# Top-6 routing of a one-core Trainium2 kernel rewritten: eight largest logits taken straight from PSUM, chosen ids marked in a row of ids, row addresses by one more top-eight

## The chip, the cores and the metric

The kernel runs on one core of one Trainium2 chip. The metric is the device time of one execution in microseconds; lower is better.

## The reference

The program is two gated blocks of two layers each, over x of shape (8, 256, 512), all in float32. The last layer is a mixture of experts, and the change is in its routing. Cut to what matters:

```python
x = x + tanh(g_xattn[0]) * retention(layernorm(x), ctx)      # stages F.*
x = x + tanh(g_ffn[0]) * dense_ffn(layernorm(x))             # stages F.*
x = x + tanh(g_xattn[1]) * attention(layernorm(x), ctx)      # stages T.*, L.*: 8 heads, softmax over 512
# the routed layer (stages R.*, L.*, then the experts); E = 64 experts, TOPK = 6, CAP = 256 rows per expert
scores = sigmoid(x_flat @ w_gate)                            # (2048, 64)
_, topk_idx = top_k(scores, 6)
w = take_along_axis(scores, topk_idx, -1); w = w / w.sum(-1, keepdims=True)
pos = (running count of earlier choices of the same expert)  # valid = pos < 256
x_disp[expert, pos] = x_flat[token]                          # dropped where pos >= 256
h = silu(g_r) * v_r;  out_r = h @ w_down[expert]
routed = sum over the 6 choices of w * out_r[expert, pos] (0 where dropped)
x = x + tanh(g_ffn[1]) * (shared_mlp(x) + routed)
```

## The kernel before, in words

Tokens come in 8 batches of 256 (two tiles of 128 partitions each). The program has three parts. `setup_and_scores` (to about 72 us in the profile) makes the retention matrix. `main_loop` (72 to 790 us) runs three pipelines over the batches at once: F (retention and dense layer), T (attention, key by key group) and R (normalisation, gate logits and routing). `experts` (790 us to the end) goes through 32 pairs of experts and then adds the results.

The order of the work on every engine is written out by hand in two tables, `ORDER` and `ENDING`. An entry `R.gates+2` in ORDER means: in step s, do stage R.gates for batch s-2. There are 7 steps, s = 0 to 6; after them ENDING lists the rest as stage/batch. Every engine walks the same list and runs the entries for which it has code, strictly in that order. So an entry's place also decides what stands behind it in each engine's queue. In step s the tables hold F for batch s, T for batch s-1 (from s = 1) and R for batch s-2 (from s = 2), so R runs inside steps 2 to 6 for batches 0 to 4; batches 5, 6 and 7 are in ENDING, and batch 7 is split into its two tiles (stages L.*).

Names that the prediction uses:
- `quad` is four PSUM banks. `T.S0` to `T.S7` write attention scores there on TensorE (line 1279), and after each one VectorE takes a maximum over 2,048 columns (`maxima`, L992, tile t_nmx). `QUADS` makes T.S(n+1) wait on TensorE until that maximum is done. `T.Q0` to `T.Q7` (L1319, L1322) write the shifted scores there again, and ScalarE takes the exponential (L791, L802).
- `T.sum0a`, `T.sum0b`, ... on GpSimd add exponentials, four additions of 128x512 each (L703, tile t_psum). Additions and indirect DMAs (`R.x0` to `R.x3`, L715, which send rows to their expert's slots in xs_d) share GpSimd's queue.
- Routing before: `R.gates` (TensorE, logits; ScalarE takes exp(-logit) over 128x128), `R.sigmoid` on VectorE (add 1, reciprocal, MAX8 and FIND_INDEX8 per tile, cast of the ids), `R.hot` (a one-hot of 6 x 64 per token by comparison with a row of ids, its sum over the six choices, the running count `cum`), `R.pos` on TensorE (prefix sums by two small matmuls per tile), `R.slots` (the one-hot times the positions, and a reduction) and `R.places` (address = a packing of expert and position, with a large number added for dropped rows; token ids; weights).
- L.* are the same stages for batch 7, one tile at a time; `L.up0` to `L.up7` (TensorE, L1186) are the shared expert's first matmuls, kept to fill the end of the main loop.

## Time and profile before

| | us |
|---|---|
| timed runs, median of 3 | 1126.71 (1125.02 to 1128.56) |
| profiled execution, first to last instruction | 1137.7 |
| TensorE busy, VectorE busy in it | 1041.9, 681.7 |
| GpSimd busy, ScalarE busy in it | 485.5, 322.6 |

The only time that the profiled execution has of its own is its span, 1137.7 us; that is 11.0 us above the median of the timed runs. The engines overlap, so their busy times do not add up to the span. PE is TensorE, PEld its weight loads, DVE VectorE, ACT ScalarE, POOL GpSimd.

### The profile page before, as it was taken

The page shows a single profiled execution, that of the slowest core. Times are in us where ns is not written, and L with a number is a line of the kernel's source. Part 1 is how long each engine was busy: PE and PEld are TensorE (multiplying, and loading weights), DVE is VectorE, ACT ScalarE, POOL GpSimd, SP SyncE. Part 2 cuts the span into 40 slices and gives each one's busy share as a digit, 9 for nine tenths or more (in the row PEclk, how much of TensorE's full clock was granted, in tenths as well). Part 3 has the DMA queues.
Part 4 walks back from the last instruction along what each step waited for, and adds up shares of the span by engine and source line. Part 5 has one row for each costly group of instructions (what it writes and reads, how often), then busy time and mean ns, then how long its engine had stood idle before and what let it go on. Part 6 is the DMA issues. An engine that isn't in the chain of part 4 may idle for free.

```text
span 1137.7 us, 16279 instructions
## 1 busy us (share of the span) xinstructions
PE 1041.9 (92%) x6109; PEld 570.0 (50%) x6110; DVE 681.7 (60%) x1290; ACT 322.6 (28%) x446; POOL 485.5 (43%) x468
## 2 busy tenths in 40 slices
PE   7988889999999999999999987789999999998586
PEld 6975544554454554545544622347555555554232
DVE  3331463778878787787788755763444444443366
ACT  3420023224133232232241321432433333333121
POOL 1100013625655665647657485054344454445100
PEclk9997999999999999999999996899999999999799
DMA  8872079579580580661603141436879999983898
GB/s 310 298 312 93 1 268 375 192 289 336 184 327 30 187 316 20 243 241 65 217 1 113 77 156 73 182 133 256 301 286 392 374 366 341 376 290 140 330 409 321
DMA packets 93786, 262.30 MB, mean 231 GB/s; under 512 B 10623, under 2 KB 10751, under 8 KB 92944
## 3 DMA queue, kind: packets, MB, share of 16 engines
q1 hardware_dynamic: 43920, 146.18, 35.1%
q10 hardware_dynamic: 31872, 63.97, 15.2%
q0 software_dynamic: 17920, 51.15, 11.5%
q8 instruction: 48, 0.79, 0.3%
q14 instruction: 26, 0.21, 0.1%
HBM read 129.91 MB, written 139.72 MB: 237 GB/s over the span
## 4 chain that ended last, share of the span: by engine, by line
PE 76%; DMA 7%; DVE 6%; issue 4%; ACT 3%; POOL 3%; another core or an unknown queue 1%; SPq 0%; POOLq 0%; ACTq 0%; DVEq 0%
PE banks L1178 18%; PE banks L1186 10%; PE banks L1687 10%; PE banks L1279 6%; PE banks L1319 6%; PE banks L1698 6%; DMA e_eo<-y_d 6%; PE banks L1673 6%; PE banks L1337 4%; DVE t_nmx L992 3%; PE banks L1200 2%; ACT t_probs L791 1%; PE banks L1172 1%; POOL t_psum L703 1%; PE banks L391 1%
## 5 line engine op out<-in xcount | busy, mean ns | idle before, releaser
L1526 POOL DMA_INDIRECT y_d<-e_eo,e_ids x128 | 124.5, 972 | 148.4 <-DVE e_eo L1615 117.2
L992 DVE TENSOR_REDUCE t_nmx<-banks 128x4 f32<-128x2048 f32 x64 | 146.4, 2288 | 55.0 <-PE banks L1279 54.9
L703 POOL TENSOR_TENSOR t_psum<-t_psum,t_probs 128x512 f32<-128x512 f32 x112 | 140.8, 1289 | 63.0 <-ACT t_probs L791 61.5
L791 ACT ACTIVATE t_probs<-banks 128x2048 f32<-128x2048 f32 x56 | 105.1, 1878 | 149.6 <-PE banks L1322 139.0
L715 POOL DMA_INDIRECT xs_d<-r_norm,r_xaddr x96 | 96.5, 1005 | 52.1 <-DVE r_xaddr L1125 26.5
L1279 PE MATMUL banks<-b_key,b_qry 32*128 32x512 f32 x512 | 77.1, 673 | 25.4 <-DVE t_nmx L992 19.0
L675 POOL TENSOR_TENSOR f_rstd<-f_veps,mhalf 128x2 f32<-128x2 f32 x24 | 16.9, 706 | 189.1 <-DVE f_veps L893 189.0
L1319 PE MATMUL banks<-b_qry,b_key 32*128 32x512 f32 x512 | 73.9, 647 | 16.0 <-ACT t_probs L791 7.3
L703 POOL TENSOR_TENSOR t_psum<-t_probs,t_probs 128x512 f32<-128x512 f32 x56 | 72.0, 1319 | 16.3 <-ACT t_probs L791 14.3
L1673 PE MATMUL banks<-ident,e_xg 128*128 128x128 f32 x512 | 70.4, 280 | 1.6 <-DMA e_xg<-xs_d 0.9
L1673 PEld LDWEIGHTS banks<-ident,e_xg 128*128 128x128 f32 x512 | 54.8, 141 | 26.2 <-issue 24.3
L1591 DVE COPY e_xT<-banks 128x512 f32<-128x512 f32 x44 | 30.4, 692 | 58.4 <-PE banks L1673 57.9
L1186 PE MATMUL banks<-f_normT,wupT 128*128 128x256 f32 x256 | 63.5, 405 | 0.0
L1178 PE MATMUL banks<-wo,f_zT 128*128 128x512 f32 x128 | 60.3, 616 | 2.4 <-issue 2.4
L1615 DVE COPY e_eo<-banks 128x512 f32<-128x512 f32 x64 | 44.3, 692 | 27.7 <-PE banks L1698 20.1
L1337 PE MATMUL banks<-t_probs,b_cT 128*32 128x512 f32 x448 | 60.6, 625 | 0.0
L1186 PE MATMUL banks<-b_xnT,wg 128*128 128x256 f32 x256 | 59.9, 389 | 0.2 <-DVE f_zT L912 0.2
L1186 PEld LDWEIGHTS banks<-f_normT,wupT 128*128 128x128 f32 x256 | 50.4, 202 | 17.6 <-issue 10.5
L1178 PE MATMUL banks<-wdnT,f_hT 128*128 128x512 f32 x128 | 58.8, 604 | 0.0
L1178 PE MATMUL banks<-wexp,f_normT 128*128 128x512 f32 x128 | 58.5, 601 | 0.0
L1546 ACT ACTIVATE e_eo<-banks 128x512 f32<-128x512 f32 x64 | 38.2, 597 | 62.7 <-PE banks L1698 43.6
L1186 PEld LDWEIGHTS banks<-b_xnT,wg 128*128 128x128 f32 x256 | 48.5, 194 | 12.4 <-issue 5.6
(217 smaller groups left out, 1653.8 us busy)
## 6 DMA issues: line engine op xcount, KB each, us to landing
xs_d<-zero ACTq DMA_DIRECT2D x32, 1056.0 KB, 9.9
e_xg<-xs_d SPq DMA_DIRECT2D x32, 1056.0 KB
y_d<-zero ACTq DMA_DIRECT2D x24, 1024.0 KB
e_xg<-y_d SPq DMA_DIRECT2D x16, 768.0 KB, 15.1
e_eo<-y_d SPq DMA_DIRECT2D x16, 768.0 KB, 14.5
wo<-in_wud SPq DMA_DIRECT2D x8, 768.0 KB
wupT<-in_wud SPq DMA_DIRECT2D x8, 768.0 KB
wdnT<-in_wud SPq DMA_DIRECT2D x8, 768.0 KB
```

The lines of the kernel that those rows point to most:

```text
L703: ins = g_.tensor_tensor(psum0[:, q, :], first[:, q, :], probs[s % NP][:, q, :], ALU.add)
L715: g_.indirect_dma_start(out=xs_d, out_offset=bass.IndirectOffsetOnAxis(ap=xaddr[b % 2][:, t, k:k + 1], axis=0), in_=normR[b % 2][:, t, :], ...
L791: A(probs[s % NP][:, :, :], quad[:, :, :], ACT.Exp, scale=SCALE1).then_inc(W["exp_ok"], 1)
L992: V.tensor_reduce(nmx[g][:, m, :], quad[:, :, :], axis=AX.X, op=ALU.max, negate=True).then_inc(W["mx_ok"], 1)
L1178: ins = mm(dst, lhs[:, k, t * P:(t + 1) * P], w[:, k, :], start=(k == 0), stop=(k == KC - 1))
L1186: ins = mm(dst[:, j * S:(j + 1) * S], w[:, k, o * P:(o + 1) * P], rhs[:, k, :], start=(k == 0), stop=(k == KC - 1))
L1279: ins = mm(quad[:, q, :], qry[b % 2][r, g, m * P:(m + 1) * P], key[b % 2][r, g, :], start=True, stop=True)
L1319: mm(quad[:, q, :], key[b % 2][r, g, n * P:(n + 1) * P], qry[b % 2][r, g, :], start=True, stop=False)
L1337: ins = mm(pV[q * HD:(q + 1) * HD, :], cT[:, n, r:r + HD], probs[s % NP][:, q, :], start=(n == 0), stop=(n == KC - 1))
L1526: g_.indirect_dma_start(out=y_d, out_offset=bass.IndirectOffsetOnAxis(ap=ids[:, HC * p + n:HC * p + n + 1], axis=0), in_=eo[u][:, n, :], i ...
L1673: last = tr(pT[t][:, k * P:(k + 1) * P], xg[u][:, HT * e + t, k * P:(k + 1) * P], ident[:, :])
L1687: last = mm(pU[j][HE * e:HE * (e + 1), 0:CAP], wu[u][:, e, k, j * HE:(j + 1) * HE], xT[p % 3][:, e, k, :], start=(k == 0), stop=(k == KC - 1))
```

## The change

It rewrites the routing stages, moves them in the two tables and changes how rows are addressed. It does the following.

- `R.sigmoid` and `R.hot` become one VectorE stage `R.top`. MAX8 and FIND_INDEX8 read the logits in PSUM (the sigmoid keeps their order, so the same six are found). The ids are cast, and MATCH_REPLACE writes -1 over the chosen ids in a row of 72 ids (64 experts and 8 fillers); "below 0" then gives the 0/1 row `chosen16`, and also `room`, a constant per expert where it is chosen. The running count is updated from `chosen16`; a third small matmul per batch replaces one of its two copies.
- `R.slots` becomes: subtract the positions from `room`, zero what does not fit, MAX8, and one tensor_scalar that turns the result into addresses. The six addresses of a token now come sorted by expert, and an expert's rows are filled in plain order (256 x expert + position) where they were interleaved in two halves.
- `R.places` goes; `R.weigh` takes exp(-x) of eight values per token (ScalarE, at R.pos), and VectorE makes sigmoid, sum and weights of those.
- Token ids are written once at the start by GpSimd (4 iotas) and raised by one VectorE instruction per batch (`next_tokens`, behind R.norm) from batch 2 on.
- In ORDER, R.top stands behind F.turn2B and ahead of T.S5; R.sigmoid had stood behind F.upA and R.hot behind F.upB. In ENDING, R.x0 and R.x1 of batch 6 both stand ahead of L.add0, and slots of tile 0 stand ahead of norm of tile 1.

```diff
-T.S5+1 R.x3+3 T.V0+1 F.logits+0 T.V1+1 F.best+0 T.S6+1 F.upA+0 R.sigmoid+2 T.S7+1 T.P1+1 F.upB+0 R.hot+2 T.Q2+1 F.weight+0 T.M1+1
+R.norm+2 F.x1b+0 T.Q0+1 R.turnA+2 F.stats2+0 R.turnB+2 R.keep+2 F.next+0 R.x2+3 T.Q1+1 T.sum0a+1 R.gates+2 F.turn2A+0 F.norm2+0 F.turn2B+0 R.top+2
+T.S5+1 R.x3+3 T.V0+1 F.logits+0 T.V1+1 F.best+0 T.S6+1 F.upA+0 T.S7+1 T.P1+1 F.upB+0 T.Q2+1 F.weight+0 T.M1+1
...
+        pool.wait_ge(at_done, 4)
+        for u in range(2):
+            g_.iota(tokk[u], pattern=[[TOPK * P, T], [1, TAG]], base=u * TOPK * S - NOWHERE, channel_multiplier=TOPK,
+                    allow_small_or_imprecise_dtypes=True).then_inc(W["zero_ok"], 1)
...
+        def next_tokens(b):
+            V.tensor_scalar(tokk[b % 2], tokk[b % 2], float(2 * TOPK * S), None, ALU.add)
...
+        def r_top(part):
+            def stage(b):
                 each, ts, n = tiles(b, part)
+                if b == 0:
+                    dve.wait_ge(W["zero_ok"], 6)
+                dve.wait_ge(W["gt_mm"], n)
+                p = lambda t: bank("R.gates", b)[:, t * E1:(t + 1) * E1] if part is None else bank(f"L.gates{t}", b)[:, 0:E1]
                 for t in each:
+                    ins = V.max(top[:, t, :], p(t))
                 link("r", ins)
                 for t in each:
+                    ins = V.max_index(topi[:, t, :], top[:, t, :], p(t))
+                ins.then_inc(W["top_ok"], 1)
+                dve.wait_ge(W["top_ok"], n)
+                link("r", V.tensor_copy(topf[b % 2][:, ts, 0:TOPK], topi[:, ts, 0:TOPK]))
+                for t in each:
+                    ins = V.match_replace(out=marked[:, t, :], in_to_replace=topf[b % 2][:, t, :], in_values=iota_e[:, :], imm_value=-1.0)
+                if part != 1:
+                    V.tensor_copy(cum16[:, :], cum[:, :])
                 link("r", ins)
+                V.tensor_scalar(chosen16[:, ts, :], marked[:, ts, 0:E1], 0.0, None, ALU.is_lt).then_inc(W["m_ok"], 1)
+                ins = V.scalar_tensor_tensor(out=room[:, ts, :], in0=marked[:, ts, 0:E1], scalar=0.0,
+                                             in1=place_e[:, :].unsqueeze(1).broadcast_to([P, len(each), E1]), op0=ALU.is_lt, op1=ALU.mult)
+                link("r", ins)
+                if part is None:
+                    for t in each:
+                        link("r", V.tensor_tensor(cum[:, :], cum[:, :], chosen16[:, t, :], ALU.add))
...
+                link("r", V.tensor_tensor(left[:, ts, :], room[:, ts, :], p, ALU.subtract))
+                V.scalar_tensor_tensor(out=slot[:, ts, :], in0=p, scalar=float(CAP), in1=left[:, ts, :], op0=ALU.is_lt, op1=ALU.mult).then_inc(W["pos_ok"], 1)
...
+                    ins = V.max(slot8[:, t, :], slot[:, t, :])
...
+                V.tensor_scalar(xaddr[u][:, ts, :], slot8[:, ts, 0:TOPK], -1.0, float(ROWS_END), ALU.mult, ALU.add).then_inc(W["route_ok"], 1)
...
+                if t == 1:
+                    mm(dst[:, t * E1:(t + 1) * E1], ones16[:, :], chosen16[:, 0, :], start=False, stop=False)
+                ins = mm(dst[:, t * E1:(t + 1) * E1], ones16[:, :], cum16[:, :], start=False, stop=True)
```

On VectorE, in a middle step of the main loop, these rows stand in the program before, from the second normalisation of F (f_norm) to the first conversion of the attention maxima (t_nmp). The three TENSOR_REDUCE rows are the maxima of T.S5, T.S6 and T.S7:

```order
L935 TENSOR_SCALAR f_norm<-f_xs_74,f_mv,f_rstd 128x512 x2
L992 TENSOR_REDUCE t_nmx<-banks 128x4
L942 MAX f_m<-banks 128x8 x2
L944 TENSOR_TENSOR f_gap<-f_m 128x2
L992 TENSOR_REDUCE t_nmx<-banks 128x4
L1066 TENSOR_SCALAR r_eg<-r_eg 128x128
L1067 RECIPROCAL r_score<-r_eg 128x128
L1069 MAX r_top<-r_score 128x8 x2
L1072 MAX_INDEX r_topi<-r_top,r_score 128x8 x2
L1074 CAST r_norm_79<-r_topi 128x2x8
L992 TENSOR_REDUCE t_nmx<-banks 128x4
```

And this stands at the same place of VectorE's queue in the changed program:

```order
L939 TENSOR_SCALAR f_norm<-f_xs_74,f_mv,f_rstd 128x512 x2
L1077 MAX r_top<-banks 128x8 x2
L1080 MAX_INDEX r_topi<-r_top,banks 128x8 x2
L1083 CAST r_norm_79<-r_topi 128x2x6
L1085 MATCH_REPLACE r_marked<-r_norm_79,iota_e 128x72 x2
L1087 CAST r_cum<-r_cum 128x64
L1089 TENSOR_SCALAR r_chosen<-r_marked 128x128
L1090 SCALAR_TENSOR_TENSOR r_room<-r_marked,place_e 128x128
L1095 TENSOR_TENSOR r_cum<-r_cum,r_chosen 128x64 x2
L996 TENSOR_REDUCE t_nmx<-banks 128x4
L946 MAX f_m<-banks 128x8 x2
L948 TENSOR_TENSOR f_gap<-f_m 128x2
```

The routing instructions moved from behind the maximum of T.S6 to the front of the maximum of T.S5, and what R.hot did later in the step now stands here too.

On GpSimd, near the end of the main loop, these rows stand in the program before, from batch 6's residual sum (r_acc_76) to batch 7's first one-tile power (r_rstd 128x1); the DMA rows send batch 6's rows to xs_d, twelve of them in all:

```order
L711 TENSOR_TENSOR r_acc_76<-f_xs_73,t_att 128x512
L680 TENSOR_TENSOR r_rstd<-r_veps,mhalf 128x2
L715 DMA xs_d<-r_norm_78,r_xaddr 16384x528 x3
L711 TENSOR_TENSOR r_acc_77<-f_xs_74,t_att 128x512
L715 DMA xs_d<-r_norm_78,r_xaddr 16384x528 x3
L685 TENSOR_TENSOR r_rstd<-r_veps,mhalf 128x1
```

In the changed program the same stretch of GpSimd's queue reads:

```order
L718 TENSOR_TENSOR r_acc_76<-f_xs_73,t_att 128x512
L687 TENSOR_TENSOR r_rstd<-r_veps,mhalf 128x2
L722 DMA xs_d<-r_norm_78,r_xaddr 16384x528 x6
L718 TENSOR_TENSOR r_acc_77<-f_xs_74,t_att 128x512
L692 TENSOR_TENSOR r_rstd<-r_veps,mhalf 128x1
```

Batch 7's first residual sum now stands behind six sends of batch 6 instead of three, and none stand between it and the power.

## Rows read from the trace of the kernel before

**Rows 1.** Page, part 1: busy us, share of the span, instructions.

```profile
PE 1041.9 (92%) x6109; PEld 570.0 (50%) x6110; DVE 681.7 (60%) x1290; ACT 322.6 (28%) x446; POOL 485.5 (43%) x468
```

**Rows 2.** Windows: stretch, length, busy by engine (instructions), granted clock, DMA share, GB/s.

```profile
359.00:437.50 78.50, 76.05 (x455) 38.75 (x453) 61.86 (x107) 22.95 (x25) 47.78 (x43) 1.00 0.50 183
640.00:645.00 5.00, 5.00 (x19) 4.03 (x16) 4.07 (x9) 0.00 (x0) 0.97 (x1) 0.66 0.27 108
757.00:790.00 33.00, 29.80 (x130) 24.87 (x130) 15.39 (x57) 5.22 (x10) 17.04 (x17) 0.90 0.50 185
790.00:1047.00 257.00, 253.43 (x1790) 141.97 (x1792) 120.48 (x295) 91.45 (x168) 117.65 (x121) 1.00 0.87 325
```

**Rows 3.** Waits of TensorE, 359.0 to 437.5 us: total, times, longest.

```profile
PE banks L1279 <- DVE t_nmx L992: 1.4, 1, 1.4
PE banks L1319 <- ACT t_probs L791: 1.0, 1, 1.0
```

**Rows 4.** Groups of VectorE by shape: count, busy us, mean ns, idle before.

```profile
L1104 DVE TENSOR_TENSOR r_ohp<-r_onehot,r_post 128x384 f32<-128x384 bf16 x16 | 19.3, 1238 | 1.4 <-DVE r_post L1101 1.4
...
L1084 DVE TENSOR_REDUCE r_chosen<-r_onehot 128x128 f32<-128x768 bf16 x7 | 10.5, 1497 | 0.2
```

**Rows 5.** Timeline, 395 to 410 us (step 4): start, us, instruction, idle before.

```profile
396.14 2.00 PE L1178 MATMUL banks<-wg,r_normT 128*128 128x64 f32 x16
...
399.56 4.94 POOL L703 TENSOR_TENSOR t_psum<-t_probs,t_probs 128x512 f32<-128x512 f32 x4
...
400.22 2.29 DVE L992 TENSOR_REDUCE t_nmx<-banks 128x4 f32<-128x2048 f32 x1 [3.67 <-PE banks L1279]
...
403.28 1.25 DVE L944 TENSOR_TENSOR f_gap<-f_m 128x2 f32<-128x2 f32 x1
403.89 1.14 PE L1279 MATMUL banks<-b_key,b_qry 32*128 32x512 f32 x8
...
405.10 2.29 DVE L992 TENSOR_REDUCE t_nmx<-banks 128x4 f32<-128x2048 f32 x1 [0.56 <-PE banks L1279]
...
408.55 0.35 DVE L1069 MAX8 r_top<-r_score 128x8 f32<-128x64 f32 x2
...
408.94 0.09 DVE L1072 MATCH_VALUE_LOAD r_topi<-r_top,r_score 128x8 f32 x1
...
409.21 0.22 DVE L1072 FIND_INDEX8 r_topi<-r_top,r_score 128x8 uint32<-128x64 f32 x1
409.46 0.17 DVE L1074 CAST r_norm<-r_topi 128x16 f32<-128x16 uint32 x1
```

**Rows 6.** Timeline, 648 to 655 us: small VectorE operations beside GpSimd's additions.

```profile
648.89 4.93 POOL L703 TENSOR_TENSOR t_psum<-t_probs,t_probs 128x512 f32<-128x512 f32 x4 [7.76 <-ACT t_probs L791]
649.34 0.90 DVE L1085 CAST r_chosen<-r_chosen 128x128 bf16<-128x128 f32 x1
650.16 1.27 DVE L1089 CAST r_cum<-r_cum 128x64 bf16<-128x64 f32 x1
...
651.35 1.33 DVE L1090 TENSOR_TENSOR r_cum<-r_cum,r_chosen 128x64 f32<-128x64 f32 x1
...
652.72 1.17 DVE L1089 CAST r_cum<-r_cum 128x64 bf16<-128x64 f32 x1
653.81 0.21 DVE L1090 TENSOR_TENSOR r_cum<-r_cum,r_chosen 128x64 f32<-128x64 f32 x1
```

**Rows 7.** Timeline, 239 to 250 us (step 2).

```profile
239.10 2.00 PE L1178 MATMUL banks<-wg,r_normT 128*128 128x64 f32 x16
...
241.25 4.95 POOL L703 TENSOR_TENSOR t_psum<-t_probs,t_probs 128x512 f32<-128x512 f32 x4 [3.14 <-ACT t_probs L791]
...
246.86 1.14 PE L1279 MATMUL banks<-b_key,b_qry 32*128 32x512 f32 x8
```

**Rows 8.** Timeline, 784 to 791 us: the end of the main loop.

```profile
789.28 0.60 ACT L867 ACTIVATE r_normT<-banks 128x512 f32<-128x512 f32 x1 [2.86 <-PE banks L1186]
...
790.12 1.06 PE L1673 MATMUL banks<-ident,e_xg 128*128 128x128 f32 x8 [0.88 <-DMA e_xg<-xs_d]
```

More of the change, by code:

```diff
@@ L31 @@
 SCALE1 = float(1.0 / np.sqrt(np.float32(HD)))
-SKIP = 1.0e6
+ROWS_END = 1 << 15
 NOWHERE = 1 << 20
@@ L442 @@
 F.turnA/7 T.V7/5 T.Z1/5 F.turnB/7 T.add1/5 T.S3/6 F.gateA/7 R.x0/4 R.stats/5 F.gateB/7 R.x1/4 T.S4/6 T.P0/6 F.keys/7 R.acc/5 F.x1a/7
-R.norm/5 T.S5/6 T.M0/6 F.x1b/7 R.turnA/5 R.turnB/5 F.stats2/7 F.next/7 R.x2/4 T.Q0/6 F.norm2/7 R.gates/5 T.S6/6 F.turn2A/7 F.turn2B/7 T.V0/6
-R.x3/4 T.sum0a/6 F.logits/7 T.S7/6 R.sigmoid/5 T.sum0b/6 T.P1/6 F.upA/7 T.Q1/6 T.sum0c/6 F.upB/7 F.best/7 T.Q2/6 R.hot/5 F.weight/7 T.M1/6
-F.expert0/7 R.slots/5 R.places/5 R.x0/5 R.pos/5 T.Q3/6 T.V1/6 F.down0/7 R.keep/5 T.Q4/6 F.expert1/7 T.Q5/6 R.x1/5 F.down1/7 T.V2/6 L.load/7
+R.norm/5 T.S5/6 T.M0/6 F.x1b/7 R.turnA/5 R.turnB/5 F.stats2/7 F.next/7 R.x2/4 T.Q0/6 F.norm2/7 R.gates/5 T.S6/6 R.top/5 F.turn2A/7 F.turn2B/7 T.V0/6
@@ L446 @@
+R.x3/4 T.sum0a/6 F.logits/7 T.S7/6 T.sum0b/6 T.P1/6 F.upA/7 T.Q1/6 T.sum0c/6 F.upB/7 F.best/7 T.Q2/6 F.weight/7 T.M1/6
+F.expert0/7 R.slots/5 R.weigh/5 R.x0/5 R.pos/5 T.Q3/6 T.V1/6 F.down0/7 R.keep/5 T.Q4/6 F.expert1/7 T.Q5/6 R.x1/5 F.down1/7 T.V2/6 L.load/7
 T.Q6/6 F.stats3/7 T.V3/6 T.Z0/6 F.norm3/7 R.x2/5 T.Q7/6 T.V4/6 T.cT/7 R.acc/6 T.A0/6 R.x3/5 L.S0/7 T.sum1a/6 T.V5/6 T.V6/6 L.S1/7 T.add0/6
-L.S2/7 L.S3/7 T.sum1b/6 L.up0/7 L.S4/7 T.V7/6 L.P0/7 T.sum1c/6 L.S5/7 T.A1/6 L.M0/7 T.add1/6 T.Z1/6 L.Q0/7 R.stats/6 R.x0/6 L.Q1/7 R.norm/6
@@ L579, in main_loop @@
     tokk = [normR[u][:, :, D + TAG:XW] for u in range(2)]
[L580 to L581 removed]
+    marked = sb("r_marked", [P, T, E1 + TAG])
     chosen16 = sb("r_chosen16", [P, T, E1], BF16)
     cum = sb("r_cum", [P, E1])
[L584 to L588 removed]
+    cum16 = sb("r_cum16", [P, E1], BF16)
+    room = sb("r_room", [P, T, E1])
+    left = sb("r_left", [P, T, E1])
+    slot = sb("r_slot", [P, T, E1])
+    slot8 = sb("r_slot8", [P, T, 8])
+    etop = sb("r_etop", [P, T, 8])
+    sig = sb("r_sig", [P, T, 8])
     wsum = sb("r_wsum", [P, 2, T])
@@ L614, in main_loop, with tiles @@
     last = lambda b, t: b + 1 + t
+    def tiles(b, t):
+        return (range(T), slice(0, T), b + 1) if t is None else ((t,), slice(t, t + 1), last(b, t))
     def load_front(sp, b):
@@ L817, in r_turn, with r_exps @@
             return stage
-        def r_gates(b):
-            act.wait_ge(W["gt_mm"], b + 1)
-            A(eg[:, :, :], bank("R.gates", b)[:, 0:T * E1].rearrange("p (t e) -> p t e", t=T), ACT.Exp, scale=-1.0).then_inc(W["eg_ok"], 1)
+        def r_exps(part):
+            def stage(b):
+                each, ts, n = tiles(b, part)
+                act.wait_ge(W["top_ok"], n)
+                A(etop[:, ts, :], top[:, ts, :], ACT.Exp, scale=-1.0).then_inc(W["etop_ok"], 1)
+            return stage
         def last_turn(t):
@@ L1047, in stage @@
                                 ALU.subtract, ALU.mult).then_inc(W["x4n_ok"], 1)
+                if t == 0:
+                    next_tokens(b)
             return stage
@@ L1132, in vector @@
                   "F.stats3": f_stats3, "F.norm3": f_norm3, "T.P0": parts(0), "T.P1": parts(1), "T.A0": attended(0), "T.A1": attended(1),
-                  "R.stats": r_stats, "R.norm": r_norm, "R.sigmoid": r_sigmoid(None), "R.hot": r_hot(None),
-                  "R.slots": r_slots(None), "R.places": r_places(None),
+                  "R.stats": r_stats, "R.norm": r_norm, "R.top": r_top(None), "R.slots": r_slots(None), "R.weigh": r_weigh(None),
                   "L.P0": parts(0), "L.P1": parts(1), "L.A0": attended(0), "L.A1": attended(1)}
@@ L1142, in vector @@
             stages[f"L.norm{t}"] = last_norm(t)
-            stages[f"L.sigmoid{t}"] = r_sigmoid(t)
-            stages[f"L.hot{t}"] = r_hot(t)
+            stages[f"L.top{t}"] = r_top(t)
             stages[f"L.slots{t}"] = r_slots(t)
-            stages[f"L.places{t}"] = r_places(t)
+            stages[f"L.weigh{t}"] = r_weigh(t)
         for n in range(KC * NG):
```

131 lines of the change are left out of this document (42 added, 89 removed), and 2 rows, old and new, of the table RELEASES.

## The prediction

> **What bounds the kernel now.** I read the page's busy times first, then the windows of single stretches, then the waits inside one step, then the timeline around the place where the routing moves to. Over the span TensorE is busy 92% and VectorE 60% [rows 1]. That average hides the stages, so the windows come next: in the step from 359.0 to 437.5 us TensorE works 76.05 of 78.50 us at the full granted clock, VectorE 61.86 [rows 2]. What is left to TensorE is 2.4 us of waits, and the list of waits names both: 1.4 us for the maximum of one quad (t_nmx) and 1.0 us for one exponential [rows 3]. Both are the round trip of a quad that TensorE has just written and needs again; neither waits for routing. In the expert stage TensorE is busy 253.43 of 257.00 us [rows 2]. So the kernel is bound by TensorE, and VectorE matters only where TensorE stands still for it.
>
> **What the change removes.** Three of the instructions that go, two products of one-hot and positions at 1,238 ns on average and one reduction at 1,497 ns [rows 4], already make 2 x 1.24 + 1.50 = 4.0 us of VectorE per batch. The rest of R.hot, R.slots and R.places adds to that. I cost this at nothing: in the middle steps TensorE hides it, with no wait for it in the list [rows 3]. If a step were bound by VectorE the same edit would be worth those 4 us and more; there is none. The large exponential on ScalarE goes and a small one comes at a place where ScalarE has idle time; also nothing. The one extra small matmul per batch (64 columns) has no row of its own; I bound it by 0 and by one sixteenth of the gate group of the same width (2.00 us for sixteen fp32 matmuls [rows 5]), 0.13 us; eight batches make 0 to 1.0 us, and I take 0.2, since nothing waits for its result.
>
> **What it moves, and what that costs.** R.top now stands ahead of the maximum of T.S5 in VectorE's queue. TensorE cannot start T.S6 until that maximum is done. The timeline of step 4 gives the room [rows 5]. The gate logits end at 396.14 + 2.00 = 398.14. The maximum of S5 ran from 400.22 for 2.29 us, to 402.51, and TensorE came to T.S6 at 403.89 without waiting. VectorE had been idle for 3.67 us before 400.22, and that gap is where R.top is put. The slack: R.top may end at 403.89 - 2.29 = 401.60, that is 3.46 us after the logits, before TensorE waits.
>
> How long is R.top on a quiet chip? Two MAX8 0.35 us (SBUF source in the row; PSUM now, taken the same). FIND_INDEX8 with its loads, twice: 408.94 to 409.43, 0.49. Cast of ids 0.17. MATCH_REPLACE is not in this trace; below nothing it cannot be, above I bound it by the FIND pair, which also loads eight values and streams a row of about this length, and take that, 0.49. Then a cast of the count, the comparison, `room` and two additions: 0.21 each by the last row of [rows 6], 1.05. With five hand-overs of 0.03 (409.43 to 409.46 [rows 5]) it is 2.7 us, ending at 400.8. That fits, with 0.8 to spare.
>
> But it is not quiet there. GpSimd's four additions of T.sum0a run from 399.56 to 404.50 [rows 5], right over the second half of R.top. What such company does to a small VectorE instruction is shown at 648.89 [rows 6]. There four additions run in 4.93 us, 1.23 us each. The cast that starts at 649.34 ends at 650.24, the next cast takes 1.27 us, an addition of 64 columns 1.33, another cast 1.17, and the same addition takes 0.21 once GpSimd has finished. So each of them passes only when one GpSimd instruction ends, one per GpSimd instruction. The f_gap row in step 4 itself (1.25 us for two columns [rows 5]) ends at 404.53, at the end of the same four additions. The maxima from PSUM are not touched: 2.29 us beside these additions.
>
> Now R.top in step 4 with this rule. MAX8, FIND, cast: 398.14 + 0.35 + 0.49 + 0.17 + 0.1 = 399.25. MATCH_REPLACE reads one row; I take it as unhindered: 399.75. The cast of the count then meets the first addition, the comparison the second, `room` the third, the first cum addition the fourth, ending at 404.50; the second cum addition is free, 0.26 with its hand-over: 404.76. The maximum of S5 ends at 407.05, TensorE starts T.S6 at 407.1 instead of 403.89. **A stall of 3.2 us.** It is robust against small shifts: there are five instructions to pass and four additions to pass them at, so one of them slipping in early changes only who is last. What is queued behind: on VectorE the maximum, then F's logits (f_gap), not needed by TensorE at once; on TensorE T.S6, the up projection, everything after. TensorE has no spare time in the step to win it back.
>
> Steps 3 to 6 have the same pattern: 4 x 3.2 = 12.8. Step 2 (batch 0) has its additions from 241.25 to 246.20, right behind logits that end at 241.10, and T.S6 at 246.86 [rows 7]. Cast of ids, cast of count, comparison and `room` each meet one; the two cum additions follow free, 0.5, so R.top ends at 246.7, the maximum at 249.0: 2.2 us. Together 15.0 us. From batch 2 on next_tokens (bounded by 0 and 0.2, the small-instruction row) stands ahead of F's statistics and moves sum0a later by as much: 3 x 0.2 = 0.6.
>
> The Trainium skill has the rule behind the row: SBUF — State Buffer, section Who interferes with whom, says that VectorE's copies, casts and tensor_scalars in a two-port mode, and any instruction with two SBUF inputs, wait for a whole GpSimd instruction, while reductions and one-input instructions outside those modes never do. By that, `room` and the comparison wait as I assumed and MATCH_REPLACE does not; the trace agrees for casts and additions, and shows nothing for the other three. Without these sentences the sum is the same.
>
> **The clock.** A stall of 3 us can also lower TensorE's granted clock. The windows show one such place: at 640 to 645 us, in the same part of a step (T.S7 and the up projection behind the narrow logits), it is 0.66 over 5 us [rows 2], which is 5 x 0.34 = 1.7 us of full-clock work lost, and that without a stall. Whether the new stall does it no row shows: 0 to 5 x 1.7 = 8.5 us. I take 3, nearer nothing, since step 4 as it stands keeps 1.00 through its own two waits.
>
> **The ends of the main loop.** Batch 5's R.top (ENDING) stands behind the maximum of T.S6; GpSimd adds only from 648.89 there [rows 6], so it runs free. For batch 7 addresses come earlier, and so do the last sends. But TensorE begins the experts at 790.12, and the last copy it also needs ends at 789.28 + 0.60 = 789.88 [rows 8]. So rows that land 2 or 3 us earlier buy 0.2 us, unless the shared matmuls in front get faster too. TensorE is idle 33.00 - 29.80 = 3.2 us in that stretch at clock 0.90 [rows 2]; I take -0.7, from 0 to -6.5 (3.2 idle and 3.3 of clock). The four iotas stand where GpSimd waits; 0. Rows in plain order in xs_d change neither bytes nor matmuls; 0.
>
> **Sum.** 15.0 + 0.6 + 0.2 + 3 - 0.7 = 18.1 us. Against the profiled execution: 1137.7 to about 1155.8. The timed runs lie 11.0 below that; the shift should carry over: 1126.7 + 18.1 = 1144.8, I say **1145 us**, slower.
>
> **Rivals.**
> (a) As above, stall of about 3 us in five steps, clock between nothing and 8.5: 1126.7 + 15.8 - 0.7 = 1142 up to 1150, with margins 1138 to 1154. Chance 0.55. For it: [rows 6] and the place in [rows 5].
> (b) Only casts and additions wait, comparison and `room` do not: then three instructions meet three additions, R.top ends near 403.3, the maximum at 405.6, a stall of 1.7 to 1.9: five make 9, 1130 to 1138. Chance 0.15. Against it: nothing direct.
> (c) No stall: VectorE gets its instructions through, or TensorE meets slack. R.top ends at 400.8, under the 401.60 that decides. What stays is the end of the loop: 1126. Chance 0.15. Against it: f_gap at the same place does wait.
> (d) Faster, the other side: no stall, and the end of the loop pays. R.top ends before 401.60, batch 7's prefix matmul finds its input ready, the shared matmuls follow without a gap and the clock stays up from 757 to 790 us: up to 6.5 us, 1120 to 1123. Chance 0.15. For it: TensorE is idle 3.2 us there. Against: the up matmuls alone fill most of it.
> A fifth case, that the change does not shorten VectorE's work, is excluded by the 4.0 us of instructions gone.
>
> **How the numbers follow.** About 0.3% (3.4 us) is what a measurement of this kernel can tell from no change. Slower by more: (a) and (b), 0.70. Within: (c), 0.15. Faster: (d), 0.15. The time is that of (a), 1145, whose own range is 1138 to 1154. The range for 8 in 10 leaves out most of (d) and what lies above 1154: 1123.5 to 1154.
>
> **What would show it.** Right: in steps 2 to 6 TensorE's wait for t_nmx (T.S6 behind T.S5) once more per step, about 3 us, at T.S6; five VectorE instructions of about 1.2 us between the gate logits and that maximum, while sum0a runs; VectorE's busy time in a step clearly down from 61.86 although the step is longer (81 to 83 us against 78.50); TensorE's start of the experts bound by the last shared copy. Wrong: R.top in under 3.4 us, steps of 78.5 us, or comparison and `room` at 0.2 beside the additions (b). What would upset all of it is GpSimd starting sum0a later than R.top ends.

## The result and the profile after the change

The changed kernel takes 1166.37 us (median of 4 runs, 1165.27 to 1167.46), the kernel before 1126.71 us in the same comparison (median of 3; a fourth execution, of 1245.04 us, was in a slow state and is left out). The ratio is 1.0355, with a 95% interval of 1.0335 to 1.0375. That is 39.7 us slower. The direction was forecast and so was the place; the size was not: 18.1 us were predicted, and 1166 lies 12 us above the top of the range.

Page of the changed kernel, part 1 (against [rows 1]):

```profile
PE 1058.5 (91%) x6117; PEld 580.6 (50%) x6118; DVE 624.6 (54%) x1216; ACT 321.6 (28%) x446; POOL 484.3 (42%) x471
```

VectorE lost 57 us of busy time, as its code lost instructions (an instruction of VectorE that is held counts as busy here, so the instructions saved more than that), and TensorE's busy time grew by 16.6 us with 8 matmuls more: the same work was done at a lower clock. The windows of the five steps that hold routing, cut at the first matmul of F.out0, show where (columns as in [rows 2]). First the changed kernel, then the control, which is the kernel before run once more:

```profile
204.11:287.70 83.59, 78.80 (x458) 40.21 (x454) 53.09 (x98) 22.84 (x25) 35.35 (x31) 0.96 0.71 265
...
373.31:458.75 85.44, 78.43 (x458) 39.94 (x454) 55.78 (x99) 22.83 (x25) 47.55 (x43) 0.96 0.46 168
...
sum 426.94, PE 393.81 PEld 200.38 DVE 277.89 ACT 114.80 POOL 227.17; mean PE 78.76 PEld 40.08 DVE 55.58 ACT 22.96 POOL 45.43
```

```profile
201.23:280.13 78.90, 76.16 (x456) 38.77 (x452) 60.49 (x107) 22.96 (x25) 35.62 (x31) 1.00 0.78 281
...
358.66:437.19 78.53, 76.08 (x456) 38.77 (x453) 61.88 (x107) 22.97 (x25) 47.83 (x43) 1.00 0.49 183
...
sum 394.57, PE 381.84 PEld 194.27 DVE 309.92 ACT 115.47 POOL 228.67; mean PE 76.37 PEld 38.85 DVE 61.98 ACT 23.09 POOL 45.73
```

Steps 2 to 6 together take 426.94 - 394.57 = 32.4 us more, 4.7 in step 2 and 6.8 to 7.1 in each of the others. In step 4 VectorE is busy for 55.78 us where it was for 61.88, and the step is longer by 6.9. The waits of TensorE in that step name the cause (against [rows 3]):

```profile
PE banks L1273 <- DVE t_nmx L996: 6.0, 2, 4.6
```

The wait for the maximum of a quad, 1.4 us before, is 6.0 now (the one for the exponential is still 1.0), 4.6 of it in one place. The timeline there (step 4, against [rows 5]):

```profile
410.54 2.00 PE L1172 MATMUL banks<-wg,r_normT 128*128 128x64 f32 x16
...
413.06 0.97 POOL L722 DMA_INDIRECT xs_d<-r_norm,r_xaddr  x1 [0.30 <-issue]
...
413.51 5.52 DVE L1083 CAST r_norm<-r_topi 128x12 f32<-128x12 uint32 x1
...
414.04 4.95 POOL L710 TENSOR_TENSOR t_psum<-t_probs,t_probs 128x512 f32<-128x512 f32 x4
...
419.34 0.22 DVE L1085 MATCH_REPLACE8 r_marked<-r_norm,iota_e 128x72 f32<-128x72 f32 x1
...
420.57 2.29 DVE L996 TENSOR_REDUCE t_nmx<-banks 128x4 f32<-128x2048 f32 x1
...
422.92 2.09 PE L1273 MATMUL banks<-b_key,b_qry 32*128 32x512 f32 x8 [4.56 <-DVE t_nmx L996]
```

One instruction does it. The cast of 12 ids, which takes 0.17 us on a quiet chip ([rows 5]), begins 0.53 us before GpSimd's four additions and ends with the last of them. The prediction had it end before them. Everything behind the cast is then quick. Behind the stall of 4.56 us the T.S6 matmuls take 2.09 us instead of 1.14, because the clock has fallen:

```profile
415.00:420.00 5.00, 3.36 (x32) 2.02 (x24) 4.97 (x8) 0.00 (x0) 4.84 (x5) 1.00 1.00 359
420.00:425.00 5.00, 2.08 (x9) 0.58 (x9) 3.08 (x7) 0.20 (x1) 2.09 (x3) 0.58 1.05 409
425.00:430.00 5.00, 5.00 (x21) 3.96 (x23) 2.29 (x1) 0.02 (x1) 0.00 (x0) 0.74 1.04 406
```

The granted clock (third column from the end) goes to 0.58 and 0.74, that is, part of the time at the lower of the two levels, 1.2 GHz, after TensorE had stood still.

Step 2 went as forecast, because there the additions run already when the cast comes:

```profile
243.48 4.96 POOL L710 TENSOR_TENSOR t_psum<-t_probs,t_probs 128x512 f32<-128x512 f32 x4 [3.13 <-ACT t_probs L798]
...
244.37 0.41 DVE L1083 CAST r_norm<-r_topi 128x12 f32<-128x12 uint32 x1
...
245.10 0.22 DVE L1085 MATCH_REPLACE8 r_marked<-r_norm,iota_e 128x72 f32<-128x72 f32 x1
...
245.96 1.34 DVE L1089 TENSOR_SCALAR r_chosen<-r_marked 128x128 bf16<-128x128 f32 x1
247.22 1.37 DVE L1090 SCALAR_TENSOR_TENSOR r_room<-r_marked,place_e 128x128 f32<-128x128 f32 x1
...
251.49 2.09 PE L1273 MATMUL banks<-b_key,b_qry 32*128 32x512 f32 x8 [2.34 <-DVE t_nmx L996]
```

Each of the cast, the count (245.24, 0.81 us), the comparison and `room` passes at the end of one addition, MATCH_REPLACE is not touched, and TensorE stalls 2.34 us.

### The profile page after: what moved, and what is told of

The parts are those of the page before. It is cut to its first block, busy times and chain, and to the rows that moved or that the text cites. A ratio compares the mean times of both kernels' runs of the same rounds, so it can differ in the third digit from the quotient of the medians.

```text
span 1165.7 us, 16200 instructions
## 1 busy us (share of the span) xinstructions
PE 1058.5 (91%) x6117; PEld 580.6 (50%) x6118; DVE 624.6 (54%) x1216; ACT 321.6 (28%) x446; POOL 484.3 (42%) x471
## 4 chain that ended last, share of the span: by engine, by line
PE 78%; DVE 10%; DMA 6%; ACT 3%; issue 2%; POOL 1%; SPq 0%; POOLq 0%; ACTq 0%; DVEq 0%
PE banks L1172 17%; PE banks L1180 13%; PE banks L1685 10%; PE banks L1273 6%; PE banks L1313 6%; PE banks L1696 6%; PE banks L1671 5%; DMA e_eo<-y_d 5%; DVE t_nmx L996 4%; PE banks L1331 3%; PE banks L1194 2%; DVE r_norm L1083 2%; ACT t_probs L798 2%; PE banks L395 1%; PE banks L389 1%
## 5 line engine op out<-in xcount | busy, mean ns | idle before, releaser
L1273 PE MATMUL banks<-b_key,b_qry 32*128 32x512 f32 x512 | 83.0, 721 | 45.5 <-DVE t_nmx L996 40.2
L1180 PE MATMUL banks<-f_normT,wupT 128*128 128x256 f32 x256 | 68.8, 429 | 0.0
L1180 PEld LDWEIGHTS banks<-f_normT,wupT 128*128 128x128 f32 x256 | 54.5, 218 | 23.4 <-issue 15.0
L1273 PEld LDWEIGHTS banks<-b_key,b_qry 32*128 32x128 f32 x512 | 21.9, 200 | 81.0 <-DVE t_nmx L996 56.3
L1613 DVE COPY e_eo<-banks 128x512 f32<-128x512 f32 x64 | 44.3, 692 | 29.4 <-PE banks L1696 29.4
```

The source lines that it names most:

```text
L1180: ins = mm(dst[:, j * S:(j + 1) * S], w[:, k, o * P:(o + 1) * P], rhs[:, k, :], start=(k == 0), stop=(k == KC - 1))
L1273: ins = mm(quad[:, q, :], qry[b % 2][r, g, m * P:(m + 1) * P], key[b % 2][r, g, :], start=True, stop=True)
```

## The experiments

**Control.** The kernel before, again. It gives the step lengths above and the spread of one execution.

> The kernel before, unchanged, as a control. Every theory expects the ratio 1.000 and, in a profile without a disturbed stretch, a span about 10 us under the 1137.7 us profiled before (in which TensorE stood still around 675 to 700 us, a stall that the changed kernel's profile does not have), steps of 78.5 us.

Measured: 1128.15 us, ratio 1.0003 [0.9979, 1.0027]; the profiled execution spans 1131.9 us. Single executions of this kernel run from 1123 to 1134 us (on the chip of one later run, from 1133 to 1150), so only differences of steps are read from single profiles below, and times from medians.

**The additions later.** In ORDER only:

```diff
-... R.x2+3 T.Q1+1 T.sum0a+1 R.gates+2 ... R.top+2 T.S5+1 R.x3+3 T.V0+1 ...
+... R.x2+3 T.Q1+1 R.gates+2 ... R.top+2 T.S5+1 R.x3+3 T.sum0a+1 T.V0+1 ...
```

> The changed kernel with GpSimd's four sum0a additions issued behind the send R.x3 in the main loop, so that the new routing stage runs beside sends alone. Theory A (the company of the four additions is what holds the new stage): the cast of the ids takes 0.2 us, the stage ends 2.7 us after the logits, steps 3 to 6 are 78 to 79 us, TensorE's clock stays at 1.00 in them, and the time is 1126 to 1132 us. Theory B (the stage is long by itself, or its place ahead of the maximum costs whatever GpSimd does): steps stay at 85 us and the time at 1160 to 1166 us. Under A a rest is possible if the additions, being later, hold something else: about 1 to 3 us per step.

Measured: 1145.89 us, ratio 1.0173 [1.0153, 1.0194]: half of the loss is gone, which is less than A had allowed for. Steps 3 to 6 are still 2.2 to 3.8 us longer than in the control, and step 2 is still 4.7 us longer: there is no send in it, so the edit changes nothing there and the stage meets the additions as before. In steps 3 to 6 the new stage is free of the additions (the ids' cast takes 0.17 us), but another instruction took its part:

```profile
407.78 5.17 DVE L948 TENSOR_TENSOR f_gap<-f_m 128x2 f32<-128x2 f32 x1
407.97 4.94 POOL L710 TENSOR_TENSOR t_psum<-t_probs,t_probs 128x512 f32<-128x512 f32 x4
...
415.20 1.67 PE L1273 MATMUL banks<-b_key,b_qry 32*128 32x512 f32 x8 [2.05 <-DVE t_nmx L996]
```

A subtraction of 2 columns asks 0.19 us before the additions and waits 5.17 us, in all four of steps 3 to 6. It now holds the maximum behind it, and TensorE 2.05 us later. So it is neither the cast nor its type: it is what GpSimd does at that moment. The cast itself begins here 0.36 to 0.46 us into a send, as it does in the changed kernel, but another send follows and not the additions, and it passes:

```profile
403.14 0.98 POOL L722 DMA_INDIRECT xs_d<-r_norm,r_xaddr  x1 [0.30 <-issue]
...
403.57 0.17 DVE L1083 CAST r_norm<-r_topi 128x12 f32<-128x12 uint32 x1
```

**The send later.** `T.Q1+1 T.sum0a+1 R.x2+3` instead of `R.x2+3 T.Q1+1 T.sum0a+1`, so that GpSimd is adding when the cast comes.

> The changed kernel with the send R.x2 issued behind the sum0a additions, so that GpSimd is already inside an addition when VectorE comes to the cast of the ids. Theory A1 (the cast waits through all four additions because it is requested just before they begin, behind a send): the cast then takes at most 1.3 us, each small instruction passes at the end of one addition, the stall is the 2 to 3.2 us per step of the prediction, steps 82 to 84 us, time 1140 to 1152 us. Theory A2 (the cast of 12 unsigned integers waits for a run of additions wherever it meets them): the cast again takes about 5 us, or what is left of the four additions, steps 84 to 86 us and 1160 to 1168 us.

Measured: 1155.27 us, ratio 1.0240 [1.0208, 1.0272]. The mechanism is A1's (the cast was held because it asked behind a send, just before the additions):

```profile
407.46 4.96 POOL L710 TENSOR_TENSOR t_psum<-t_probs,t_probs 128x512 f32<-128x512 f32 x4 [2.69 <-ACT t_probs L798]
...
408.28 0.48 DVE L1083 CAST r_norm<-r_topi 128x12 f32<-128x12 uint32 x1
409.21 0.81 DVE L1087 CAST r_cum<-r_cum 128x64 bf16<-128x64 f32 x1
```

The same cast takes 0.48 us, the comparison and `room` behind it 1.34 and 1.37, one to an addition. The stall at T.S6 is 2.33 to 2.35 us in steps 2 to 6, and steps 3 to 6 are 82.5 to 84.2 us, as expected. The time came out 3 us above the range: the five steps are 22.5 us longer than the control's, and the rest of the 29.4 us (against 1125.83) lies outside them and is not explained. The edit changes two things at once: the cast asks during the first addition, and no send stands directly ahead of the additions any more. This run is the prediction's own mechanism, one instruction to an addition. Of its 22.5 us, 11.7 are stalls and 10.8 come on top of them.

**One cast alone.** The kernel before with a stage of constant data at the new stage's place; its own routing untouched:

```diff
+        def r_probe(b):
+            dve.wait_ge(W["gt_mm"], b + 1)
+            for t in range(T):
+                ins = V.max(q_m[:, t, :], iota_e[:, :])
+            link("r", ins)
+            for t in range(T):
+                ins = V.max_index(q_i[:, t, :], q_m[:, t, :], iota_e[:, :])
+            link("r", ins)
+            link("r", V.tensor_copy(q_f[:, :, :], q_i[:, :, 0:TOPK]))
```

> The kernel before, with four instructions more on VectorE where the changed kernel has its routing stage (behind the gate logits, ahead of the maximum of T.S5): two top-eights, two searches for ids and ONE cast of 12 unsigned integers, all of constant data; its own routing is untouched. Theory A (a two-port instruction that asks for SBUF while the last send of GpSimd runs and four additions stand right behind it waits for all four): the cast takes 5.5 us in steps 3 to 6, TensorE then waits 4.0 to 4.6 us for the maximum, and with the clock's share steps are 84 to 85 us: this one cast makes the kernel 1150 to 1158 us. Theory B (the loss of the changed kernel is made by the whole stage, by its ten or so instructions one after another): a single cast costs at most 1.3 us, which the slack holds: steps 78.5 to 79 us, 1126 to 1129 us.

Measured: 1152.33 us against 1128.01, ratio 1.0205 [1.0181, 1.0229], +24.3 us.

```profile
402.27 5.41 DVE L1140 CAST q_f<-q_i 128x12 f32<-128x12 uint32 x1
402.70 4.94 POOL L704 TENSOR_TENSOR t_psum<-t_probs,t_probs 128x512 f32<-128x512 f32 x4
...
410.06 2.09 PE L1290 MATMUL banks<-b_key,b_qry 32*128 32x512 f32 x8 [2.91 <-DVE t_nmx L993]
```

One cast, held in steps 3 to 6, costs 24 us, where the whole change costs 39.7. The stall was 2.91 to 3.13 us where 4.0 to 4.6 was expected, for want of the 1.5 us of small work that stands behind the cast in the changed kernel. Step 2 is as before (78.90 us): there the cast takes 0.50 us and the slack holds it.

**The same cast 0.9 us earlier.** The same stage without the two top-eights and searches.

> The kernel before with the one cast of 12 unsigned integers again at the place of the new routing stage, but without the top eights and the searches ahead of it, so that it asks 0.9 us earlier: about 1.3 us before the first of the four additions, at the end of the send before the last or between the two. Theory A (only a request that comes within the last send, after GpSimd has the additions next, is held for all four): the cast takes 0.2 us, or up to 0.5 if it meets a send, steps 3 to 6 are 78.5 us, 1124 to 1131 us, ratio 0.998 to 1.003. Theory B (whoever asks while GpSimd sends is held until its additions are over): the cast takes 6 to 7 us, the steps are 84 us and the time 1150 us. That is the same instruction as in the run with the cast alone, 0.9 us earlier.

Measured: 1143.15 us against 1140.50 for the kernel before on that chip, ratio 1.0015 [0.9979, 1.0051]: no change.

```profile
394.88 0.97 POOL L717 DMA_INDIRECT xs_d<-r_norm,r_xaddr  x1 [0.31 <-issue]
395.76 0.17 DVE L1137 CAST q_f<-q_i 128x12 f32<-128x12 uint32 x1 [1.64 <-PE banks L1186]
396.16 0.97 POOL L717 DMA_INDIRECT xs_d<-r_norm,r_xaddr  x1 [0.30 <-issue]
397.14 4.95 POOL L705 TENSOR_TENSOR t_psum<-t_probs,t_probs 128x512 f32<-128x512 f32 x4
```

It asks inside a send and passes at once, 1.38 us before the additions. In step 3 it asks 0.26 us before the end of that send, takes 0.26 us and ends with it. So a send can hold a cast to its own end, but not beyond it when another send follows. In step 2, where GpSimd is idle, the cast asks only 0.11 us before the additions, and passes too:

```profile
238.76 0.17 DVE L1137 CAST q_f<-q_i 128x12 f32<-128x12 uint32 x1 [1.99 <-PE banks L1186]
...
238.87 4.95 POOL L705 TENSOR_TENSOR t_psum<-t_probs,t_probs 128x512 f32<-128x512 f32 x4 [3.14 <-ACT t_probs L793]
```

So neither a send alone nor nearness to the additions alone holds a request for 5 us. What the held requests of steps 3 to 6 share is a send with the additions directly behind it.

**Does the end of an instruction let it in?** Two versions of the changed kernel: a memset of one column ahead of the additions, and a hand-over between them.

```diff
+                if n == 1 and g == 0:
+                    g_.memset(q_t[:, :], 0.0)
```

```diff
                     ins = g_.tensor_tensor(psum0[:, q, :], first[:, q, :], probs[s % NP][:, q, :], ALU.add)
+                    if n == 1 and g == 0 and q < G - 1:
+                        ins.then_inc(W["q_add"], 1)
+                        pool.wait_ge(W["q_add"], (G - 1) * b + q + 1)
```

> The changed kernel with a memset of one element per partition on GpSimd between the send and the first of the four additions. Theory A1 (what matters is that the additions stand directly behind the send; a GpSimd instruction's end lets VectorE in): the cast passes behind the memset or the first addition, 0.5 to 2 us, and the others one per addition, as in the run with the send moved back: steps 82 to 83.5 us, 1148 to 1157 us. Theory A2 (whoever asks before a run of back-to-back GpSimd instructions waits for the whole run): the cast again takes about 5.6 us, steps 85.5 us, 1166 us.

> The changed kernel with a hand-over between the four additions of sum0a (each raises a semaphore that GpSimd itself waits for before the next), so that they are no longer back to back. Theory A3 (a request that came before the run waits because no gap opens in it): the cast passes at the first gap, about 1.8 us after its start, and the rest one per addition: steps 82 to 84 us. Theory A4 (the request waits for something else, such as the last addition's own end): the cast still takes 5.5 us or slightly more, steps 85.5 to 86 us, 1166 to 1170 us.

Measured: with the memset 1166.23 us (1.0325 [1.0301, 1.0348]); with the hand-overs 1159.16 us (1.0273 [1.0242, 1.0305]). First the one, then the other:

```profile
414.32 5.54 DVE L1086 CAST r_norm<-r_topi 128x12 f32<-128x12 uint32 x1
414.81 0.12 POOL L711 MEMSET q_t<- 128x1 f32 x1
414.87 4.94 POOL L713 TENSOR_TENSOR t_psum<-t_probs,t_probs 128x512 f32<-128x512 f32 x4
```

```profile
408.49 1.86 DVE L1086 CAST r_norm<-r_topi 128x12 f32<-128x12 uint32 x1
409.01 5.32 POOL L710 TENSOR_TENSOR t_psum<-t_probs,t_probs 128x512 f32<-128x512 f32 x4
```

The end of the memset did not let the cast in: it waits through all five, as A2 says. (The memset's record ends 0.06 us after the first addition's begins, so there was no gap at that end.) With gaps of some 0.12 us ((5.32 - 4.95) / 3) it passes at the first, as A3 says. So this cast needs a gap in the run of additions.

Is that because it asked early, or because the additions stand directly behind a send? The versions so far changed both together. The profile of the version with the cast 0.9 us earlier has a place, near the end of the main loop, that parts them:

```profile
679.99 0.97 POOL L717 DMA_INDIRECT xs_d<-r_norm,r_xaddr  x1 [0.30 <-issue]
680.98 4.92 POOL L705 TENSOR_TENSOR t_psum<-t_probs,t_probs 128x512 f32<-128x512 f32 x4
681.31 5.16 DVE L1023 SCALAR_TENSOR_TENSOR t_att<-t_att,tg_x,r_ohp 128x512 f32<-128x512 f32 x1
```

This instruction, 0.79 us at a free place of the control, asks 0.33 us after the first addition has begun, and still all four end before it does. In step 3 of the control, f_gap asks 3.55 us into such a run, 0.2 us before the third addition ends, and is held to the end of the fourth (1.44 us). So asking early is not what matters. Nothing that waited got in between additions that stand directly behind a send. The runs of additions that let one instruction in at each end (step 2, the send later, [rows 6]) all stand behind a wait for ScalarE. No run was made to test this, and t_att is the only request of its kind early in such a run.

With the hand-overs the steps did not shorten as I had expected, 85.2 us against 82 to 84, since the small instructions behind the cast then meet the remaining additions; the stall is 3.79 us instead of 4.56, and the lowered clock behind it costs 85.2 - 78.5 - 3.8 = 2.9 us instead of 2.3. Steps 2 to 6 are 31.6 us longer than the control's with them and 31.0 with the memset, so the 7 us between the two times lie outside these steps and are not won by the hand-overs.

**The stall without contention.** The kernel before, with reductions of a constant row at that place:

```diff
+            for c in range(13):
+                ins = V.tensor_reduce(q_m[:, c // 8, c % 8:c % 8 + 1], v["zero"][:, 0:512], axis=AX.X, op=ALU.max)
```

> The kernel before with thirteen reductions of a constant 512-column row on VectorE (about 0.6 us each by the rate of the t_nmx row, 7.8 us together) at the place of the new routing stage, and nothing else: one-input reductions, which in the rows so far were not held by GpSimd. It makes the maximum of T.S5 late by 3.5 to 5 us in steps 2 to 6 with no contention in it. Theory A (a stall of this length at this place costs itself and then 1 to 3 us of lowered clock): each step is longer by the stall of T.S6 plus 1 to 3 us, together 25 to 38 us, 1150 to 1165 us; the T.S6 matmul behind the stall takes 2.09 us instead of 1.14. Theory B (the surplus over the stall in the changed kernel comes from the contention and not from the clock): each step is longer by the stall alone, 17 to 25 us in all.

Measured: 1162.07 us against 1127.33, ratio 1.0306 [1.0266, 1.0345].

```profile
410.72 7.80 DVE L1135 TENSOR_REDUCE q_m<-zero 128x1 f32<-128x512 f32 x13 [1.62 <-PE banks L1185]
...
412.12 4.96 POOL L704 TENSOR_TENSOR t_psum<-t_probs,t_probs 128x512 f32<-128x512 f32 x4
...
420.90 2.09 PE L1286 MATMUL banks<-b_key,b_qry 32*128 32x512 f32 x8 [4.40 <-DVE t_nmx L993]
422.92 5.30 PE L1193 MATMUL banks<-f_normT,wupT 128*128 128x256 f32 x16
```

The reductions run 0.60 us each, right through the additions. The stall is 4.40 us, and the step grows from 78.53 to 85.53 us, by 7.0: 2.6 us come on top of the stall without any contention (2.5 to 3.2 in the five steps). Theory A holds. The T.S6 matmuls lose 2.09 - 1.14 = 0.95 and the up projection 5.30 - 3.72 = 1.58, 2.5 together. The window shows the level, 0.50 throughout, which is 1.2 GHz:

```profile
420.00:425.00 5.00, 4.10 (x13) 2.24 (x14) 3.10 (x5) 0.20 (x1) 0.79 (x1) 0.50 1.05 415
```

**Marking elsewhere.** The changed kernel with R.top cut in two: top eight and ids stay, the rest is a stage of its own behind F.upB.

```diff
+                if part is not None:
+                    r_mark(part)(b)
+            return stage
+
+        def r_mark(part):
...
-T.P1+1 F.upB+0 T.Q2+1 F.weight+0
+T.P1+1 F.upB+0 R.mark+2 T.Q2+1 F.weight+0
```

> The changed kernel with only the top eight and their ids left ahead of the maximum of T.S5, and the marking of the chosen ids, the count, the comparison and the room moved behind the up projection, where the old kernel made its one-hots. Theory A (the place of the small instructions beside the additions): steps 3 to 6 at 78 to 79 us, time 1124 to 1130 us, since less VectorE work is left than before. Theory B (the new way of routing costs by itself): still 1155 to 1166 us. If even the top eight ahead of the maximum cost TensorE time, 1 us per step and 1131 us.

> The split version once more (top eight and ids ahead of the maximum, the marking behind the up projection), because its profile showed the steps of before to 0.05 us and yet it was timed 0.7% slower, with a lowered clock (0.86) from 150 to 175 us, where no routing runs. Theory C (a disturbance of the clock early in the program that comes and goes between executions of one kernel): this time the ratio is anywhere from 0.998 to 1.007 and the profile may show 75.5 us for the first step instead of 77.6. Rival (the split costs by itself): again 1.005 to 1.009, and a place in the profile that is longer than in the version whose additions wait for f_gap.

Measured: ratio 1.0069 [1.0049, 1.0090] at first, 1.0016 [0.9995, 1.0037] the second time (1133.90 and 1129.65 us). Steps 2 to 5 take 78.53 to 78.56 us both times. The first time was above the 1130 us that A allowed. The first profile has a first step of 77.64 us instead of 75.5, with a granted clock of 0.51 from 160 to 165 us, ahead of all routing; the second has not. A second such place lies 120 us behind the last F.out0, where the first shows a clock of 0.50 over 10 us (716.57 to 726.57) and the second 0.85 (713.85 to 723.85). That is Theory C: the clock differs between two executions of one kernel. What the split itself costs lies within the second interval, and none of steps 2 to 5 is longer for it.

**Additions behind f_gap.** The version with the later additions, and GpSimd waiting for f_gap:

```diff
                 if n == 1:
+                    if g == 0 and b < NB - 2:
+                        pool.wait_ge(W["gap_ok"], b + 2)
                     since(pool, W["z_mm"], 2 * b + g)
```

> The changed kernel with the four sum0a additions behind the send R.x3 and, in addition, behind the end of f_gap (GpSimd waits for that semaphore), so that neither the routing stage nor the top eight of the narrow logits asks for SBUF ahead of them. Theory A: the cast takes 0.2 us, f_gap 0.2 us instead of 5.2, no new wait of TensorE for t_nmx, steps 3 to 6 at 78.5 us, step 2 at 79, time 1126 to 1131 us, and within 0.3% of before if the clock stays up. Rival: GpSimd, later by a microsecond or two, becomes late for sum0b or the divisor, and the steps stay at 80 us or more (1136 us and up).

Measured: 1129.28 us against 1128.01, ratio 1.0021 [0.9996, 1.0046]: the whole new routing, at the old speed within what the interval tells. Page and step 4:

```profile
PE 1035.7 (92%) x6117; PEld 569.1 (51%) x6118; DVE 599.4 (53%) x1216; ACT 321.5 (29%) x446; POOL 483.5 (43%) x471
```

```profile
356.56:435.11 78.55, 76.10 (x458) 38.80 (x454) 50.40 (x99) 22.83 (x25) 47.49 (x43) 1.00 0.49 183
```

VectorE has 82 us less to do than in the kernel before ([rows 1]), 11.5 us less in this step ([rows 2]), and the step is 78.55 us long instead of 78.5.

**And the ending.** That version with `R.top/5 T.S6/6` instead of `T.S6/6 R.top/5`, and the last tile's normalization ahead of the first tile's slots.

> The version whose additions wait for f_gap, with two places of the ending changed as well: R.top of batch 5 ahead of the maximum of T.S6 (so that the bank of the narrow logits comes free 0.9 us after the gate logits and not behind that maximum), and the last tile's normalization ahead of the first tile's slots, as before the change. Theory: TensorE's wait for the ids ahead of the narrow logits (1.3 us) goes, and with it some of the clock loss behind it (the matmul of T.S7 took 2.09 us there instead of 1.14, the up projection 5.93 instead of 3.72); the wait for r_norm falls from 1.5 to 0.8. Together 2 to 5 us less than the version without: 1123 to 1127 us, ratio 0.996 to 1.000. Rival: the maximum of T.S6, now behind 2.7 us of routing, holds T.S7 as long as the logits were held, and nothing is won: 1.001 to 1.003.

Measured: 1131.03 us, ratio 1.0023 [1.0001, 1.0044]: nothing won, where 1123 to 1127 us was expected. The number is the rival's, but its mechanism is not seen: T.S7 is not held. At the place itself it does what it should (version without, then with):

```profile
636.24 2.04 PE L1174 MATMUL banks<-wg,f_normT 128*128 128x8 f32 x16 [1.29 <-DVE r_topi L1082]
...
640.23 5.93 PE L1182 MATMUL banks<-f_normT,wupT 128*128 128x256 f32 x16
```

```profile
639.21 1.95 PE L1174 MATMUL banks<-wg,f_normT 128*128 128x8 f32 x16
...
643.22 4.49 PE L1182 MATMUL banks<-f_normT,wupT 128*128 128x256 f32 x16
```

The wait for the ids is gone, and the T.S7 matmuls between the rows take 2.02 us instead of 2.09. From the gate logits to the second up projection it is 648.92 - 634.00 = 14.9 us instead of 647.37 - 629.66 = 17.7. But the profiled execution lost more later, 120 us behind the last F.out0, in a stretch of 10 us: the clock there is 0.87 without (713.79 to 723.79) and 0.50 with (716.69 to 726.69). But it is 0.50 in the changed kernel and in the control too, and the two executions of the split version differ there in the same way (0.50 and 0.85). So this loss can't be laid to the edit. The transfer of the first expert rows added a wait of 2.2 us. Whether a local gain of 2.8 us is there in the median is open: the two medians, 1129.28 and 1131.03 us, come from different chips.

## Why the prediction was wrong in size

The time is 39.7 us up where 18.1 were forecast. Of the 21.6 us that were missing, 5.7 are the stalls (20.7 instead of 15.0), 8.7 the clock behind them (11.7 instead of 3) and 7.2 lie outside the five steps. Two steps of the prediction failed: it let the ids' cast pass ahead of the additions, and it took the clock near nothing.

- **What bounds the kernel; removed work costs and brings nothing.** Right. 82 us of VectorE time went in the version with the additions behind f_gap, for a ratio of 1.0021.
- **R.top on a quiet chip, 2.7 us.** Right: 2.6 us for batch 5, 673.97 to 676.58.
- **"MAX8, FIND, cast: ... = 399.25".** This step failed, and the stalls came out 5.7 us longer with it. The cast of the ids was costed at 0.17 us because it should end before the additions (399.56). It did ask before them, by 0.53 us, and was held until the last had ended: 5.52 us. The rule taken from [rows 6], one small instruction per GpSimd instruction, is right for additions that stand behind a wait for ScalarE, as those of [rows 6] do (step 2, and the version with the send later). In steps 3 to 6 the additions stand directly behind a send, and nothing got in between them. [rows 5] could not tell the two apart: f_gap asks there when the last addition is about to begin. The sentence that the stall "is robust against small shifts" was wrong with it: for one cast, asking 0.9 us earlier decides between 24 us and none.
- **The stall.** Predicted 3.2 us in steps 3 to 6 and 2.2 in step 2; measured 4.66, 4.56, 4.57 and 4.56, and 2.34. By all waits for t_nmx at this line it is 40.2 us against 19.5 in the control, 20.7 instead of 15.0.
- **The clock.** This step failed too, and by more: 3 us taken, 8.5 as bound; measured 32.4 - 20.7 = 11.7 us over five steps, 2.3 each. It would have failed with the stalls right: in the version with the send later, whose stalls are 2.33 to 2.35 us, 10.8 us come on top. In step 4 it is 0.95 in T.S6 and 5.01 - 3.72 = 1.29 in the up projection. The run without contention gives 2.6 for a stall of nearly the same length (4.40 us), so this belongs to the stall and not to the contention. The rows of step 4 before, with waits of 1.4 and 1.0 us at a full clock, said nothing about a longer one.
- **Comparison and `room` wait, MATCH_REPLACE does not.** Right (1.34, 1.37, 0.22 us). That excludes rival (b). Rival (c) needed a stage that nothing holds; the version with the additions behind f_gap is what it describes.
- **Loop end, -0.7 us.** Bound by the last shared copy, as said, with no gain; and a wait was overlooked: the narrow logits of batch 7 wait 1.3 us for a bank that R.top now frees behind the maximum of T.S6. Rival (d) fails too: without any stall (additions behind f_gap) the ratio is 1.0021.
- **What remains.** 39.7 - 32.4 = 7.3 us outside steps 2 to 6, by the medians. The wait of 1.3 us may be one part of it, though the version with the additions behind f_gap has it too and is not slower. The two profiled executions show less, (1165.7 - 1131.9) - 32.4 = 1.4 us, but the control's lasted 1133.59 us and so 5.4 more than its median. Single executions of kernels that are equally fast differ by as much outside these steps, and I leave it open.

The Trainium skill (SBUF — State Buffer, section Who interferes with whom) says that issue order decides who blocks and that the first holds the shared ports for the whole instruction. The trace agrees with the classes: reductions pass beside additions at 0.60 us, casts and two-input additions do not. It does not agree with the extent: the held cast had its start recorded 0.53 us before the additions, and still it waited for four of them (for five instructions with the memset), not one. Why nothing gets in between additions directly behind a send, while something does at each end behind a wait for ScalarE, no run here shows.

## What to carry to other kernels

Before a small instruction is put ahead of a critical one, read what the other engine on its ports does at that very moment, and with how much margin: a run of back-to-back additions directly behind a send cost a request the whole run (5.5 us), a run behind a wait for ScalarE cost it one addition, and asking 0.9 us earlier cost nothing. Price a new stall on a saturated TensorE with the clock behind it. Here 2.2 to 3.2 us came on top of stalls of 4.4 to 4.7 us, and hardly less, 1.4 to 3.0, on top of stalls of 2.3 to 3.1. Behind stalls of 2.0 to 2.1 us (the additions later, steps 3 to 6) it was 1.8 us twice and nothing twice. And if two runs on different engines must not meet, say so with a semaphore (the additions waiting for f_gap): moving one of them by a place in the list only chose another victim.
